# Source logits of the first softmax by matching products, W1 prepared beside the strips of x, row statistics gathered in the layers

## What is computed

```python
N, E, D = 10000, 10000, 768            # nodes, edges; edges are sorted by dst
# src, dst: the edges, and a loop at each node
def gat(x, W, a_src, a_dst, b, heads, d_out, concat):
    h = (x @ W).reshape(N, heads, d_out)
    as_n = einsum('nhd,hd->nh', h, a_src); ad_n = einsum('nhd,hd->nh', h, a_dst)
    e = leaky_relu(as_n[src] + ad_n[dst], 0.2)
    ex = exp(e - segment_max(e, dst)[dst])
    alpha = ex / (segment_sum(ex, dst)[dst] + 1e-16)
    out = segment_sum(alpha[:, :, None] * h[src], dst)
    return (out.reshape(N, heads * d_out) if concat else out.mean(axis=1)) + b
h = elu(gat(layernorm(x), W1, ..., heads=4, d_out=512, concat=True))     # W1: 768 x 2048
x = x + gat(h, W2, ..., heads=1, d_out=768, concat=False)                # W2: 2048 x 768
x = x + ffn(layernorm(x))                                                # 768 -> 96 -> 768
```

## Time and profile before

| | |
|---|---|
| median of 3 runs | 4134.23 us (4128.42 to 4136.31) |
| the profiled execution | 4133.69 us, span 4131.5 us |
| mean granted TensorE clock | 0.936 of full speed |
| TensorE busy | 3564.0 us, 86% |
| VectorE busy | 2453.4 us, 59% |
| ScalarE busy | 1493.2 us, 36% |
| GpSimd busy | 769.9 us, 19% |

### The profile page before, as it was taken

How to read it: one execution, slowest core, us unless ns; L and a number is a source line. 1 busy time by engine, 2 the same in 40 slices (tenths; PEclk the granted TensorE clock), 3 DMA queues, 4 the chain that set the end, 5 groups by cost and what they waited for, 6 DMA issues and landing times. The chain is left out here.

```text
span 4131.5 us, 67733 instructions
## 1 busy us (share of the span) xinstructions
PE 3564.0 (86%) x21732; PEld 2132.1 (52%) x21733; DVE 2453.4 (59%) x5875; ACT 1493.2 (36%) x2447; POOL 769.9 (19%) x1196
## 2 busy tenths in 40 slices
PE   5930039999999999999999999999999996398888
PEld 2410025566556555655665565566556655265655
DVE  6667165556545654555565556545554634699998
ACT  1302024434433443343344334433443433144444
POOL 0148600001000000000010000000000100266665
PEclk9965559999999999999999999999999998699999
DMA  7622011111111111111111111111111100378787
GB/s 216 166 73 64 3 41 41 43 55 41 38 49 40 50 36 57 36 44 43 52 46 39 48 39 47 38 58 35 45 42 48 48 24 15 88 212 237 231 235 210
DMA packets 149563, 307.02 MB, mean 74 GB/s; under 512 B 86459, under 2 KB 86537, under 8 KB 144395
## 3 DMA queue, kind: packets, MB, share of 16 engines
q1 hardware_dynamic: 119096, 211.16, 17.1%
q0 software_dynamic: 29056, 93.03, 8.5%
q10 hardware_dynamic: 1175, 0.07, 0.0%
HBM read 266.71 MB, written 93.94 MB: 87 GB/s over the span
## 5 line engine op out<-in xcount | busy, mean ns | idle before, releaser
L1448 PE MATMUL lay_pm<-lay_zh,w1h 128*128 128x500 f16 x1920 | 718.6, 374 | 23.6 <-DVE lay_h L1312 13.0
L1450 PE MATMUL lay_pm<-lay_zh,w1l 128*128 128x500 f16 x1920 | 718.8, 374 | 0.0
L1449 PE MATMUL lay_pm<-lay_zl,w1h 128*128 128x500 f16 x1920 | 718.8, 374 | 0.0
L1124 POOL DMA_INDIRECT lay_raw<-in_x_dram,lay_idx x200 | 209.7, 1049 | 2551.8 <-PE lay_pz L1413 1634.0
L1366 ACT ACTIVATE lay_ex<-lay_pm,b1c,scale 128x500 f32<-128x500 f32 x320 | 245.4, 767 | 830.8 <-PE lay_pm L1450 830.8
L1472 PE MATMUL lay_pm<-w2h,lay_gh 128*128 128x512 f16 x1280 | 485.0, 379 | 0.0
L1472 PE MATMUL lay_pm<-w2h,lay_gl 128*128 128x512 f16 x1280 | 483.9, 378 | 0.0
L1472 PE MATMUL lay_pm<-w2l,lay_gh 128*128 128x512 f16 x1280 | 483.4, 378 | 0.0
L1357 ACT ACTIVATE lay_rows_hi<-lay_raw,lay_bias,lay_scale 128x768 f16<-128x768 f32 x200 | 205.1, 1025 | 681.7 <-DMA lay_raw<-in_x_dram,lay_idx 681.7
L1266 DVE TENSOR_SCALAR lay_ex<-lay_ex,scale 128x500 f32<-128x500 f32 x320 | 153.7, 480 | 490.3 <-ACT lay_ex L1366 487.9
L1349 ACT ACTIVATE lay_zh<-lay_pz 128x400 f16<-128x400 f32 x600 | 296.4, 503 | 232.2 <-PE lay_pz L1413 228.5
(11 more groups left out here) (319 smaller groups left out, 5981.1 us busy)
## 6 DMA issues: line engine op xcount, KB each, us to landing
x<-in_x_dram SPq DMA_DIRECT2D x20, 1500.0 KB, 6.7
out_x<-x SPq DMA_DIRECT2D x100, 288.0 KB
out_own<-h SPq DMA_DIRECT2D x100, 288.0 KB
out_dram<-out_x SPq DMA_DIRECT2D x100, 288.0 KB
lgt_x<-in_x_dram SPq DMA_DIRECT2D x20, 1344.0 KB
h<-lay_h SPq DMA_DIRECT2D x80, 336.0 KB
lgt_w<-in_L_gnn_W_dram SPq DMA_DIRECT2D x6, 1024.0 KB, 13.8
sm_wraw<-in_L_gnn_W_dram SPq DMA_DIRECT2D x6, 1024.0 KB
```

The source lines that it names most:

```text
L1124: nc.gpsimd.indirect_dma_start(raw[:, i % 2, :], None, io["x"][:, :], bass.IndirectOffsetOnAxis(ap=idx[:, i:i + 1], axis=0), bounds_check= ...
L1448: pe.matmul(o, c.w1h[:, d, cols], zh[:, d, h], start=(d == 0), stop=False)
L1449: pe.matmul(o, c.w1h[:, d, cols], zl[:, d, h], start=False, stop=False)
L1450: ins = pe.matmul(o, c.w1l[:, d, cols], zh[:, d, h], start=False, stop=(d == DC - 1))
```

## The change

- **sm1.** The four source values of an edge come by `Match`, with 316 outcomes to a column, and only the 79 gathers by destination are left on GpSimd. The class that stands beside the match, `SecondWeights`, has W2 alone. It is loaded at the stage's start. Its products with a2 are made by TensorE between the steps of the match (32 halves, each three transposes, a copy by ScalarE and three matmuls of two columns), and the maximum over W2 stands in VectorE's row at the match's chunk 40 (`TOP_AT`). Scales and the two float16 parts of W2 stand behind the match, ahead of the sums and the scans.
- **stage_logits.** `FirstWeights` has W1, which is loaded once instead of twice, and stays for the split. The count of edges is in ten parts at strips 2 to 11, the window starts at strip 12, the maxima of W1 at 13 and 14, its scale at 15, and the high and low parts at strips 16 to 19. `copy_lines` goes from VectorE to ScalarE. The hardware loop is written out. Mean and reciprocal deviation get a table of their own, `stat`, with two more stores a strip.
- **stage_layers.** The records no longer hold the statistics (12 values instead of 16), and SyncE's strided load of a strip's own statistics is gone. Ten indirect gathers from `stat` stand behind the second row gather of a strip on GpSimd, and the scale and bias are made from them by `row_scales` at chunk 8 (`SCALES_CHUNK`). `EARLY_ROWS` is {9: 0, 11: 1}. In the first strip two gathers stand ahead of the row gathers and eight behind the second. The rare extra chunks gather one more time each.
- **Scans, both softmaxes.** The gates' edges are turned once ahead of the scans; the copies of edges and carries, one of two transposes, and the clearing of spare tiles are left out.

The diff, cut to its core (lines of "..." stand for what is left out):

```diff
@@ stage_logits, VectorE and ScalarE @@
             def step(s, b, j):
                 if within(s + 1):
                     statistics(s + 1, (b + 1) % NB, j + (b + 1) // NB)
-                if within(s - 1):
-                    copy_lines(s - 1, (b - 1) % NB)
                 if within(s - 2):
                     finish(s - 2, (b - 2) % NB, j - (b < 2))
                 if within(s + 1):
                     refine(s + 1, (b + 1) % NB)
+                first.beside(dve, s)
...
+            def copy_lines(s, b):
+                act.wait_ge(dots_done, s + 1)
...
+                nc.scalar.activation(lines[:, b % 2], pl[b % 2][:], ACT.Copy).then_inc(lines_ready, 1)
@@ FirstWeights @@
+        self.raw = c.w2[:].rearrange("p a k n -> p (a k n)").bitcast(F32)[:, 0:DC * DH]
...
+        if 2 <= s < 2 + self.COUNTS:
+            self.edges_before(s - 2)
...
+        if s == self.COUNTS + 2:
+            self.window_starts(dve)
+        if 13 <= s < 15:
+            for i in (2 * (s - 13), 2 * (s - 13) + 1):
+                step = DC * DH // PIECES
+                ch.put(nc.vector.tensor_reduce(self.highest[:, i:i + 1], self.raw[:, i * step:i * step + step], AX.X, ALU.max,
+                                               apply_absolute_value=True))
+        if s == 15:
...
+            self.scales.vector(dve, ch)
+        if 17 <= s < 20:
+            for i, hi, lo, raw in part_pieces(*self.flat, self.raw):
+                if min(i, 2) == s - 17:
+                    dve.wait_ge(self.hi, i + 1)
...
@@ SecondWeights @@
+    def vector_beside(self, dve, chunk):
+        if chunk == self.TOP_AT:
...
+    def vector(self, dve):
...
+        dve.wait_ge(self.w2_summed, self.HALVES)
...
+        self.scales.vector(dve, ch)
...
+    def turn(self, pe, u):
+        if u < self.HALVES:
+            k, half = u // 2, u % 2
+            if half == 0:
+                pe.wait_ge(self.w2_in, 16 * KC)
...
@@ Match, TensorE @@
             ins.then_inc(self.spread_done, 1)
+            if self.beside:
+                self.beside.turn(pe, 2 * i)
+                self.beside.products(pe, 2 * i - 1)
             if i:
                 look(i - 1)
...
@@ stage_layers @@
             def gather(q, first):
+                def statistics(lo, hi):
+                    for i in range(lo, hi):
+                        nc.gpsimd.indirect_dma_start(stat[:, i, :], None, dr.stat[:, :], bass.IndirectOffsetOnAxis(
+                            ap=idx[:, i:i + 1], axis=0), bounds_check=N - 1, oob_is_err=False).then_inc(stat_in[i >= 2], 16)
...
                 for i in range(WPS):
+                    if i == 2:
+                        statistics(2 if first else 0, WPS)
...
+            def row_scales(qc, q, lo, hi):
+
+                dve.wait_ge(stat_in[lo >= 2], 16 * (hi - lo) * (q + 1))
...
                     if k == WEIGHTS_CHUNK:
                         weights(qc, q)
+                    if k == SCALES_CHUNK:
+                        row_scales(qc, q, 0, 2)
+                        row_scales(qc, q, 2, WPS)
```

More of the change, by code:

```diff
@@ L51 @@
 XE = 64
-REC = 16
+REC = 12
 MAX_CHUNKS = E // XE + 1
@@ L405, in step @@
                     turn(s, b, t, j)
-                    if t == 0 and not within(s, 2) and s == 1:
+                    if t == 0 and s == 1:
                         vector_sums()
+                    if t == 0:
+                        first.tensor(pe, s)
                     if t == 0 and within(s, 1):
```

615 lines of the change are left out of this document (335 added, 280 removed).

## The result

In its first four runs the changed kernel took 4291.95 us in the median (4275.44 to 4304.55), against 4133.8 for the kernel before (four runs, 4128.42 to 4136.31). The ratio is 1.0381, with an interval of 1.0363 to 1.0400. The forecast was 4084 with a range of 4042 to 4120, so the measured time lies 172 us above the upper end, and its sign is wrong.

A forecast was written before the change was run, and what follows sets the result against it. Gathers on GpSimd were taken to bound the first softmax, TensorE the logits and layers. From 4133.7 us, +11 (logits) - 96 (first softmax) - 4.4 (second) + 2.3 + 38 (layers) = -49 gave 4084, range 4042 to 4120.

The forecast's parts named there:

- (d): First softmax: the 79 gathers by destination end at T0 (stage start) + 109 + 2.3 us, hidden behind other work.
- E: Layers: VectorE's two-input elu work stretches each second small gather, 19 x 9.3 = 176 us, total 4222; chance 0.05.
- Logits, +11: Logits stage: VectorE bounds ten strips at 9.95 us a step; +11 us, bounds +3 and +14.
- First softmax, -96: First softmax: 194 us instead of 290.1 with the match replacing the source gathers; bounds -58 and -114.
- (a): First softmax: W2 must be loaded before TensorE's first transpose, so the match starts at T0 (stage start) + 27 us.
- (b): First softmax: match, 16 items 82 us, cold start 6, maximum over W2 12, last chunks 16; ends T0 (stage start) + 144.
- rival B: First softmax: match at TensorE's lower clock, 7.5 us an item, +38, total 4122; half if only W2's maximum; chance 0.13.
- (c): First softmax: the rest of W2 behind the match, copies, scale chain, high and low parts, bias; ends T0 (stage start) + 165.
- rival F: First softmax: still bound by stretched gathers, ending T0 (stage start) + 176; gives back 11 of 96, total 4095; chance 0.10.
- (e): First softmax: scans to the record's store take 24.8 us instead of 33.05, ending T0 (stage start) + 190.
- Layers, +2.3 and +38: Layers: unhidden small gathers in the first strip, +2.3; 19 strips wait 2.0 us each for statistics, +38, bounds 0 and 60.
- p: Layers: pitch of one small gather in a strip, taken as 1.44 us; the look-up is late by 9p - 11.0.

The follow-up runs named there:

- the later runs: The changed kernel, unaltered, run again beside the kernel before on four chips: 4111.32, 4102.69, 4114.49 and 4108.92 us.
- The last experiment: Maximum over W2 in four quarters (chunks 10, 22, 34, 46), against the changed kernel with scales two chunks later: 4090.60 us beside 4090.01.

## Why the prediction was right or wrong

The first runs first. The step of the prediction that failed there is the overlap. It had the 79 gathers hidden beside the match (d), and the ten of a strip cost only what VectorE waits for them; what they do to TensorE's signals was put at nothing. Measured were 297.6 us for the first softmax, where the sum has 194, and 150.3 for a strip, where the sum has 144. Why is open. None of the rivals holds 4292 either. E was the nearest in place (gathers in a strip, 19 times) and sign, 4222. Its mechanism was wrong: the gathers were not stretched. They lie 1.32 us apart in the first run's strips, and 1.31 in its first softmax. What came late was TensorE's signals to the others, which no row of the kernel before hints at.

Against the later runs each term has an answer. The sum there is -30 by the profiled spans (4101.3 against 4131.5) and -25 by the medians; the forecast was -49, and its range, 4042 to 4120, holds the medians of all four chips.

**Logits, +11: measured +9.6** (256.4 for 246.8; by the very first instruction of the next stage it is 8.5, and the first softmax then has 1.2 us more). The mechanism is the forecast one: ten steps of VectorE, from 61.0 to 160.2, take 9.92 each, forecast 9.95. TensorE's last strips go at 8.93 and not 9.38, which gives a little back.

**First softmax, -96: measured -79** (211.0 for 290.1); in the other three later profiles, -75 to -85.

(a) W2 was in at T0 + 26.4, forecast 27. TensorE, waiting for it ahead of its first transpose:

```profile
282.83 0.90 PE L678 MATMUL sm_turned<-ident,sm_wraw 128*128 128x128 f32 x3 [12.37 <-DMA sm_wraw<-in_L_gnn_W_dram]
```

(b) The match is the step that failed, by 18 us: its last pick stands at T0 + 161, forecast 143 to 144 (155 to 165 in the other three). The sizes of an item were right, but not how many go at the lower level. Two items of the match in the later run of the unaltered kernel, at the lower level and at the upper one; between two such rows lie 7.64 us (288.98 to 296.62; forecast 7.5) and 5.38 (344.30 to 349.68; forecast 5.1):

```profile
288.98 3.35 PE L853 MATMUL sm_rows<-sm_tab,sm_one 128*128 128x316 bf16 x12
...
296.62 3.60 PE L853 MATMUL sm_rows<-sm_tab,sm_one 128*128 128x316 bf16 x12
```

```profile
344.30 0.97 PE L853 MATMUL sm_rows<-sm_tab,sm_one 128*128 128x316 bf16 x6
...
349.68 0.97 PE L853 MATMUL sm_rows<-sm_tab,sm_one 128*128 128x316 bf16 x6
```

Its clock and VectorE's maximum, with the look-up that waits behind it:

```profile
290.00:310.00 20.00, 18.93 (x95) 13.49 (x94) 10.79 (x23) 5.32 (x10) 15.17 (x16) 0.56 0.07 3
310.00:350.00 40.00, 33.27 (x248) 24.00 (x247) 26.18 (x56) 15.26 (x30) 30.81 (x31) 0.91 0.08 5
350.00:392.00 42.00, 27.19 (x135) 19.79 (x134) 27.79 (x33) 8.11 (x16) 12.16 (x13) 0.59 0.03 1
```

```profile
351.14 13.01 DVE L636 TENSOR_REDUCE sm_highest<-sm_wraw 128x1 f32<-128x12352 f32 x1
```

```profile
364.65 0.97 PE L853 MATMUL sm_rows<-sm_tab,sm_one 128*128 128x316 bf16 x3 [13.19 <-DVE sm_picked L792]
```

The granted clock over the whole match is 0.73 (0.71 to 0.77 in the other three), where the prediction's sign was over 0.75. The 13.0 of the maximum and its 13.19 us of standstill came as forecast. By VectorE's picks, which stand four to an item, the 16 items take 116.0 us with it, where the sum had 82 + 6 + 12 = 100. Six of them go at the lower level, at 7.2 to 7.9 us: three at the start, as forecast (7.4 more than warm ones, for 6), and three behind the maximum, which I had at the upper level: 8 us. The ten others take 5.7 in the mean and not 5.1 (6 us), since TensorE waits a little longer in each for ScalarE's copy and VectorE's picks. The chunks behind the last item take 18.4 for 16: they go at the forecast 1.05 each, but 19 of them are left there and not 15. That is the 18. Which items go slow differs from run to run: on two chips three items of 7.9 us and three of 6.6 stand ahead of the maximum. So rival B was half right in its smaller form, the maximum alone lets the clock fall; I had priced that at 19 and it costs 8. The last experiment adds that the clock can fall in the match without the maximum too, for which no run here shows the reason.

(c) W2's parts behind the match: 418.72 to 439.7, 21.0 us, forecast 21. (d) The 79 gathers end at T0 + 109.4, forecast 109 + 2.3; none was stretched to over 1.27 us (mean 1003 ns where the gathers before had 1101 by destination and 1399 by source), so rival F has no place. (e) From the sums to the record's store:

```profile
439.71 0.73 DVE L984 TENSOR_TENSOR sm_raw<-sm_gsrc,sm_gdst 128x316 f32<-128x316 f32 x1
...
442.28 0.96 DVE L993 TENSOR_TENSOR_SCAN sm_a<-sm_pen_f,sm_l 128x79 f32<-128x79 f32 x4
...
445.90 0.96 DVE L993 TENSOR_TENSOR_SCAN sm_b<-sm_pen_l,sm_a 128x79 f32<-128x79 f32 x4
```

The wait of 86.45 in the earlier trace rows is gone, and the sums start without one. One scan and its carry take 3.62 (442.28 to 445.90), where 5.44 less 1.74 makes 3.70. The whole of it is 23.9 (to T0 + 207.2), forecast 24.8. (f) The tail is 3.8, forecast 4.

**Second softmax, -4.4: measured -5.3** (105.6 for 110.9, to the output stage's first instruction; the prediction's 104.4 ended 6.7 us earlier, with the last computation). Right in the sum; its parts were not measured one by one.

**Layers, +2.3 and +38: measured +44** (2960.3 for 2916.0). The sum is nearly right and the parts are not. What I took for all of it, the wait for the masks, is 0.60 us a strip, 11 in all, forecast 2.0 and 38. The gathers of one strip and the end of it:

```profile
1443.40 1.00 POOL L1229 DMA_INDIRECT lay_stat<-stat,lay_idx  x1 [0.30 <-issue]
...
1455.51 1.00 POOL L1229 DMA_INDIRECT lay_stat<-stat,lay_idx  x1 [0.30 <-issue]
```

```profile
1457.99 0.17 DVE L1303 SCALAR_TENSOR_TENSOR lay_scale<-lay_rel,lay_stat 128x8 f32<-128x8 f32 x1 [3.01 <-DMA lay_stat<-stat,lay_idx]
...
1460.39 0.27 PE L1527 MATMUL lay_look<-lay_slots,lay_mask 128*128 128x5 f32 x1 [0.65 <-DVE lay_mask L1318]
```

The chain is the forecast one: last statistics, scales, elu, masks, look-up. But p is 1.345 (12.11 us over nine), not 1.44, and the landing 2.48 and not 2.3. These two would make 9 x 1.345 - 11.0 + 0.18 = 1.3, so the masks' slack is 0.7 longer than I read it. I took p from the two row gathers, which move 3 KB a row. The small ones, at a mean of 1037 ns, are nearer to the 1.00 of the earlier trace rows.

The Trainium skill, SBUF — State Buffer, section "Who interferes with whom", says that VectorE's two-input operations were not seen to hold up descriptor generation, and would have left p at 1.30 and the wait at 0.7 a strip; the measured 1.345 and 0.60 are nearer to that than to my 1.44 and 2.0, the 0.60 in part by the luck of the longer slack. Its rule is not the whole, though: single gathers beside the elu took up to 1.28 us, and the one at 258.30 before took 2.89.

The other part was not in the prediction: at the head of 17 of the strips TensorE stands for 1.29 us in the mean with no engine to wait for.

```profile
1414.94 0.37 PE L1571 MATMUL lay_pm<-lay_zh,w1h 128*128 128x500 f16 x1 [1.46 <-DVE lay_h L1435]
...
1417.86 0.39 PE L1572 MATMUL lay_pm<-lay_zl,w1h 128*128 128x500 f16 x1 [1.27 <-issue]
```

That is 22 of the 44 us. It lies among loads of instructions, of which the changed program does more; the queue's lines (packets, MB, share of 16 engines) of the kernel before and of the changed one:

```profile
q8 instruction: 102, 1.67, 0.2%
q14 instruction: 134, 1.10, 0.1%
```

```profile
q8 instruction: 218, 3.57, 0.4%
q14 instruction: 53, 0.43, 0.0%
```

The loads of the first queue are 16 KB each, about four in a strip of the kernel before and ten in one of the changed kernel. The wait stands 17 times in every later run of it and its variants (1.22 to 1.45 us in the mean; 1.18 in the first run). The kernel before has no such wait, and with ten unused gathers it has none either, so it isn't the gathers. That TensorE waits for its own instructions fits the records, but no run took the loads away: argued, not shown. The remaining 11 us were not taken apart.

**Output.** 568.0 for 567.8, as forecast by leaving it out.

With the late updates aside, the step that failed is a size, that of the match. The forecast missed by 19 (by the spans) to 27 us (by the medians): 18 of it in the match and 4 in the layers. The chance of 0.90 for faster agrees with the runs on four later chips and not with the first four runs. Of the cases, the later times lie between the forecast and B.

## What to carry to other kernels

A median of four runs in one place said 3.8% slower, and four later chips said 0.5 to 0.8% faster. Before an edit is explained or thrown away on such a result, run the unaltered kernel a second time beside the edits, on the same chip: it was the one run here that turned two apparent gains of 190 and 100 us into a gain of some 11 and a loss of some 81. In a trace, look for waits that end with no work in between and at even intervals (here 8.40 us), which are not the engines' work, and compare how many landings are on record with 16 for each gather: a trace that lacks them is disturbed itself. And where TensorE stands idle or waits in turns, cost the stage at both of its levels and count which items fall under each, instead of charging the lower one to the start alone.

## What the hardware showed that I had not expected

- In the one trace kept of the first four runs TensorE's semaphore updates reached the others up to 42.05 us late while GpSimd issued indirect gathers back to back, for a while one per 8.40 us; with the end of the row (79 gathers, or 12) or 6 us behind it they were prompt again. That trace has 168 of 1264 landings of the long row on record. In the later traces the updates took 0.01 to 0.02 us, beside the same rows of gathers too.
- Small gathers beside VectorE's work on the match, which has one input in SBUF and one in PSUM, took 1.003 us in the mean; those beside the elu took 1.037, single ones 1.28.
- The granted clock was 0.54 in a stretch where TensorE was busy for 36.70 of 40 us, with bf16 and float32 matmuls of 2 to 316 columns (175 of them), and 0.91 in the same stretch of another run with 33.27 us busy and 248 matmuls.
- A longer loop body had 1.29 us of standstill on TensorE in 17 strips, beside ten loads of instructions a strip in place of four; that the loads make it is not shown.
